# State-space phase: the time steps' two-part weights as one 40-column operand, B by C moved and masked straight from PSUM, one gate product in y's banks

## The reference, cut to what matters

```
proj   = h @ in_proj_w                       # 1024 gate, 1024 ssm, 8 dt, 128 B, 128 C columns
x      = silu(causal_conv4(ssm) + conv_bias) # 8 heads of 128
dt     = softplus(dt_raw + dt_bias);  log_a = -exp(A_log) * dt      # per token and head
L[i,j] = exp(cum[i] - cum[j]) for j <= i, else 0;   CB[i,j] = C[i] . B[j]
y[i]   = sum_j L[i,j] CB[i,j] dt[j] x[j]  +  exp(cum[i]) C[i] @ state
state  = exp(total) state + sum_j exp(total - cum[j]) dt[j] B[j] x[j]
out    = residual + ((y + D x) * silu(gate)) @ out_proj_w
```

## Time and profile before

| | us |
|---|---|
| median of 3 runs | 2466.27 (2464.72 to 2467.67) |
| profiled execution, own time | 2461.78 |
| profiled execution, span from first to last instruction | 2459.9 |
| TensorE busy | 2352.0 (96%) |
| VectorE busy | 1419.1 (58%) |
| ScalarE busy | 957.4 (39%) |
| GpSimd busy | 668.4 (27%) |
| mean granted TensorE clock | 0.985 of full |

### The profile page before, as it was taken

One profiled execution on the slowest core, in us unless ns is written; L12 is line 12 of the kernel. 1 busy time (PEld: TensorE's weight loads), 2 busy tenths in 40 slices (PEclk: granted clock), 3 DMA queues, 4 the chain that ended last, 5 costly groups with the idle time before them and its releaser, 6 DMA issues. The chain is left out here.

```text
span 2459.9 us, 41911 instructions
## 1 busy us (share of the span) xinstructions
PE 2352.0 (96%) x16736; PEld 2074.3 (84%) x16736; DVE 1419.1 (58%) x3237; ACT 957.4 (39%) x1665; POOL 668.4 (27%) x526
## 2 busy tenths in 40 slices
PE   6999999999998999999999999995999999999996
PEld 5999997777787888888888999884999998777775
DVE  5767762222238777777777777765676763222221
ACT  4233332322346444455455555543333231233220
POOL 1244443111121222222222322220144444111121
PEclk9999999999999999999999999997999999999998
DMA  7644225787763111111111111004163413777868
GB/s 250 203 140 155 73 71 174 231 248 235 242 150 104 27 27 27 27 27 26 27 36 35 27 35 27 10 9 158 69 214 105 145 54 104 230 240 230 232 168 171
DMA packets 102754, 292.82 MB, mean 119 GB/s; under 512 B 22498, under 2 KB 22754, under 8 KB 91872
## 3 DMA queue, kind: packets, MB, share of 16 engines
q1 hardware_dynamic: 55216, 198.87, 23.1%
q0 software_dynamic: 47344, 91.27, 16.4%
HBM read 197.28 MB, written 151.80 MB: 142 GB/s over the span
## 5 line engine op out<-in xcount | busy, mean ns | idle before, releaser
L1714 DVE SCALAR_TENSOR_TENSOR m_xt<-m_ssm,m_convw,m_xt 128x256 f32<-128x256 f32 x384 | 219.8, 585 | 57.6 <-ACT m_ssm L1302 48.5
L1425 PE MATMUL m_p_ab<-m_ht_hi,m_wi_b_hi 128*128 128x256 f32 x640 | 183.0, 286 | 3.0 <-ACT m_gate L1274 3.0
L1427 PE MATMUL m_p_ab<-m_ht_hi,m_wi_b_lo 128*128 128x256 f32 x640 | 181.3, 283 | 0.0
L1426 PE MATMUL m_p_ab<-m_ht_lo,m_wi_b_hi 128*128 128x256 f32 x640 | 180.2, 282 | 0.0
L392 POOL DMA_INDIRECT slot_rows<-a_hr,a_slot_now x128 | 130.8, 1022 | 142.3 <-PE p_gate_a L622 85.7
L392 POOL DMA_INDIRECT slot_rows<-b_hr,b_slot_now x128 | 130.5, 1019 | 142.9 <-PE p_gate_b L622 82.8
L620 PE MATMUL p_gate_a<-a_hts_hi,a_w_hi 128*128 128x256 f32 x512 | 148.4, 290 | 7.6 <-DVE a_hts_lo L881 7.4
L620 PE MATMUL p_gate_b<-b_hts_hi,b_w_hi 128*128 128x256 f32 x512 | 148.4, 290 | 7.5 <-DVE b_hts_lo L881 7.4
L620 PE MATMUL p_up_a<-a_hts_hi,a_w_hi 128*128 128x256 f32 x512 | 148.5, 290 | 0.0
L620 PE MATMUL p_up_b<-b_hts_hi,b_w_hi 128*128 128x256 f32 x512 | 148.4, 290 | 0.0
L622 PE MATMUL p_gate_a<-a_hts_hi,a_w_lo 128*128 128x256 f32 x512 | 145.9, 285 | 0.0
(11 more groups left out here) (354 smaller groups left out, 7464.5 us busy)
## 6 DMA issues: line engine op xcount, KB each, us to landing
a_ew<-in_ew SPq DMA_DIRECT2D x32, 1536.0 KB, 7.7
b_ew<-in_ew SPq DMA_DIRECT2D x32, 1536.0 KB, 7.7
after_ffn<-a_zeros POOLq DMA_DIRECT2D x6, 2048.0 KB
out<-b_zeros POOLq DMA_DIRECT2D x6, 2048.0 KB
slot_rows<-a_zeros POOLq DMA_DIRECT2D x1, 8336.0 KB, 40.6
a_rows<-slot_rows SPq DMA_DIRECT2D x32, 260.5 KB, 8.9
b_rows<-slot_rows SPq DMA_DIRECT2D x32, 260.5 KB, 9.0
a_xr<-in_x SPq DMA_DIRECT2D x8, 1024.0 KB, 9.5
```

Source lines behind the costliest of these rows:

```text
L1425: t.matmul(out, l_hi, r_hi_, start=first, stop=False)
L1426: t.matmul(out, l_hi, r_lo_, start=False, stop=False)
L1427: return t.matmul(out, l_lo, r_hi_, start=False, stop=last)
L1714: ins_ = v.scalar_tensor_tensor(xt[:, m, :], ssm[:, m, i:i + BM], convw[:, m, i:i + 1], xt[:, m, :], ALU.mult, ALU.add)
```

## The change

- The weights of dt lie in one operand `w_dt` of 40 columns: high parts in columns 0 to 7, low parts in columns 32 to 39, zeros between (set once by ScalarE in `early`). `project_dt` makes two passes per k-step, with `ht_hi` and with `ht_lo`, 8 matmuls in place of 12. The result has 40 rows, and so has `dtt`.
- `to_tokens` turns dt to tokens by a plain fp32 product with the constant `picks` (40 rows by 8 columns, ones at h and 32 + h), which adds high and low part; the two products stand ahead of the transposes of B and not behind them.
- `b_by_c` stands directly behind `cumulate`, writes into the first bank of `p_y`, and waits for the y of the block before to be read. It is no job any more (21 jobs). VectorE masks it straight from PSUM into `cb`, behind `cum_lo`; ScalarE's copy is gone. `by_cb` and the first `y_product` wait for `cb_ready`.
- Gate 4 goes into the second bank of `p_y`; the other gates alternate in `p_ab` as before. The first `y_product` waits until gate 4 is emptied.
- VectorE's `add_state` of chunk 0 stands ahead of `gated` of chunk 0 and not behind it. For chunk 1 the order stays.

```diff
@@ -1028,10 +1028,13 @@
...
-    JOBS = 6 + 2 * CI
-    J_DT, J_C, J_B, J_TOK, J_CUM, J_CB = 0, 1, 2, 3, 6, 8
-    J_SSM = [4, 5, 7, 9, 10, 11, 12, 13]
-    J_GATE = list(range(14, 22))
+    JOBS = 5 + 2 * CI
+    J_DT, J_C, J_B, J_TOK, J_CUM = 0, 1, 2, 3, 6
+    J_SSM = [4, 5, 7, 8, 9, 10, 11, 12]
+    J_GATE = list(range(13, 21))
+    IN_X, IN_Y = [J_GATE[2], J_GATE[3]], [None, J_GATE[4]]
+    RING = [job for job in range(JOBS) if job not in IN_X + IN_Y]
...
@@ -1043,7 +1046,9 @@
...
-        wi_a = sb("wi_a_hi", [P, KD, SPLIT_COL], F32R), sb("wi_a_lo", [P, KD, SPLIT_COL], F32R)
+        wi_a = sb("wi_a_hi", [P, KD, SPLIT_COL - NH], F32R), sb("wi_a_lo", [P, KD, SPLIT_COL - NH], F32R)
+        w_dt = sb("w_dt", [P, KD, CR], F32R)
...
@@ -1055,7 +1060,7 @@
...
-        dtt = sb("dtt", [NH, BM])
+        dtt = sb("dtt", [CR, BM])
...
@@ -1097,25 +1102,33 @@
...
+            if first == DT0:
+                return w_dt[:, :, 0:NH], w_dt[:, :, LO_AT:CR]
             if first < SPLIT_COL:
-                return [part[:, :, first:first + n] for part in wi_a]
+                return [part[:, :, first - NH:first - NH + n] for part in wi_a]
             i, at = divmod(first - SPLIT_COL, 2 * P)
             return [part[:, i, :, at:at + n] for part in wi_b]
...
-        ab_of = lambda job: p_x[:, job % 2, :] if job in J_GATE[2:4] else p_ab[:, job % 2, :]
+        def ab_of(job):
+            for bank, jobs in ((p_x, IN_X), (p_y, IN_Y)):
+                if job in jobs:
+                    return bank[:, jobs.index(job), :]
+            return p_ab[:, RING.index(job) % 2, :]
...
@@ -1276,7 +1289,7 @@
...
-                copy_job(n, J_DT, dtt[:, :], NH)
+                copy_job(n, J_DT, dtt[:, :], CR)
...
@@ -1320,8 +1333,6 @@
...
                 ssm_job(2)
-                wait(act, decay_ready, n * TM)
-                copy_job(n, J_CB, cb[:, :, :])
...
@@ -1380,6 +1391,8 @@
...
                     act.wait_ge(small_loaded, 96)
                     a.activation(a_neg[:], a_neg[:], ACT.Exp).then_inc(a_exp, 1)
+                    a.activation(w_dt[:, :, NH:LO_AT], c.ones[:, 0:LO_AT - NH].unsqueeze(1).to_broadcast([P, KD, LO_AT - NH]),
+                                 ACT.Copy, scale=0.0).then_inc(gap_set, 1)
...
@@ -1438,19 +1451,34 @@
...
             def ab(n, job):
-                if job in J_GATE[2:4]:
+                if job in IN_X:
                     wait(pe, out_ready, n * TM)
+                elif job in IN_Y:
+                    wait(pe, y_read, n * TM)
                 else:
-                    before = job - 4 if job in J_GATE[4:6] else job - 2
-                    if n * JOBS + before >= 0:
-                        pe.wait_ge(ab_free, n * JOBS + before + 1)
+                    at = RING.index(job)
+                    before = n * JOBS + RING[at - 2] - (JOBS if at < 2 else 0)
+                    if before >= 0:
+                        pe.wait_ge(ab_free, before + 1)
                 return ab_of(job)
-            def project(n, job, col, width=P):
+            def project_dt(n):
                 if is_(n, 0):
-                    pe.wait_ge(w_lo_done, 1 if col == DT0 else (col - NH) // (2 * P) + 2)
-                out = ab(n, job)[0:width, 0:BM]
-                hi, lo = wi(col, width)
+                    pe.wait_ge(w_lo_done, 1)
+                    pe.wait_ge(gap_set, 1)
+                out = ab(n, J_DT)[0:CR, 0:BM]
+                for k in range(KD):
+                    for part in (ht_hi, ht_lo):
+                        mm = t.matmul(out, w_dt[:, k, :], part[:, k, :], start=(k == 0 and part is ht_hi),
+                                      stop=(k == KD - 1 and part is ht_lo))
+                mm.then_inc(ab_full, 1)
+            def project(n, job, col):
+                if is_(n, 0):
+                    pe.wait_ge(w_lo_done, (col - NH) // (2 * P) + 2)
+                out = ab(n, job)[:, 0:BM]
+                hi, lo = wi(col, P)
                 for k in range(KD):
                     mm = three(out, hi[:, k, :], lo[:, k, :],
...
@@ -1460,11 +1488,11 @@
                 pe.wait_ge(ab_free, n * JOBS + J_B + 1)
                 out = ab(n, J_TOK)
                 for j in range(TM):
-                    t.matmul(out[:, j * P:(j + 1) * P], bt[:, j * P:(j + 1) * P], c.ident[:],
-                             is_transpose=True, start=True, stop=True)
+                    at = TM * P + j * NH
+                    t.matmul(out[:, at:at + NH], dtt[:, j * P:(j + 1) * P], c.picks[0:CR, :], start=True, stop=True)
                 for j in range(TM):
-                    at = TM * P + j * NH
-                    mm = t.matmul(out[:, at:at + NH], dtt[:, j * P:(j + 1) * P], c.ident[0:NH, 0:NH],
+                    mm = t.matmul(out[:, j * P:(j + 1) * P], bt[:, j * P:(j + 1) * P], c.ident[:],
                                   is_transpose=True, start=True, stop=True)
                 mm.then_inc(ab_full, 1)
...
@@ -1480,11 +1508,13 @@
...
             def b_by_c(n):
-                out = ab(n, J_CB)
+                if n == 0:
+                    pe.wait_ge(prior.acc_ready, NS * TS)
+                wait(pe, y_read, n * TM)
                 for j in range(TM):
                     tokens = slice(j * P, (j + 1) * P)
-                    mm = t.matmul(out[:, tokens], bt[:, tokens], ct[:, tokens], start=True, stop=True)
-                mm.then_inc(ab_full, 1)
+                    mm = t.matmul(p_y[:, 0, tokens], bt[:, tokens], ct[:, tokens], start=True, stop=True)
+                mm.then_inc(cb_full, 1)
...
@@ -1518,8 +1548,9 @@
                 pe.wait_ge(decay_ready, n * TM + j + 1)
                 pe.wait_ge(cdec_ready, n * TM + j + 1)
                 pe.wait_ge(state_ready, n * TM + j + 1)
-                if n == 0:
-                    pe.wait_ge(prior.acc_ready, NS * TS)
+                if j == 0:
+                    pe.wait_ge(ab_free, n * JOBS + J_GATE[4] + 1)
+                    pe.wait_ge(cb_ready, n + 1)
                 wait(pe, y_read, n * TM + j)
...
@@ -1554,7 +1585,7 @@
             def head(n):
                 pe.wait_ge(ht_ready, n * 2 + 2)
-                project(n, J_DT, DT0, NH)
+                project_dt(n)
                 project(n, J_C, C0)
                 project(n, J_B, B0)
...
@@ -1564,10 +1595,10 @@
                 ssm_part(0)
                 ssm_part(1)
                 cumulate(n)
+                b_by_c(n)
                 if not is_(n, 0):
                     out_product(n - 1, 1)
                 ssm_part(2)
-                b_by_c(n)
                 spread(n, 0)
...
@@ -1692,8 +1723,9 @@
...
             def mask_cb(n):
-                dve.wait_ge(ab_free, n * JOBS + J_CB + 1)
-                link(v.tensor_tensor(cb[:], cb[:], c.upto[:].unsqueeze(1).to_broadcast([P, TM, P]), ALU.mult))
+                dve.wait_ge(cb_full, n + 1)
+                v.tensor_tensor(cb[:], p_y[:, 0, 0:TM * P].rearrange("p (j t) -> p j t", j=TM),
+                                c.upto[:].unsqueeze(1).to_broadcast([P, TM, P]), ALU.mult).then_inc(cb_ready, 1)
...
@@ -1704,6 +1736,7 @@
...
             def by_cb(n, j):
+                dve.wait_ge(cb_ready, n + 1)
                 dve.wait_ge(decay_exp, n * TM + j + 1)
...
@@ -1801,10 +1834,10 @@
...
                     ends(n)
                     cum_lo(n)
+                    mask_cb(n)
                     if n > 0:
                         add_out(n - 1, 1)
                     convolve(n, 2)
-                    mask_cb(n)
                     differences(n, 0)
...
@@ -1828,8 +1861,8 @@
...
                     skip_part(n, 0)
+                    add_state(n, 0)
                     gated(n, 0)
-                    add_state(n, 0)
                     halves(n, 0)
```

More of the change, by code:

```diff
@@ L1112, in mamba @@
         small_loaded, w_hi_done, w_lo_done = sem("small_loaded"), sem("w_hi_done"), sem("w_lo_done")
-        a_exp, set_up = sem("a_exp"), sem("set_up")
+        a_exp, set_up, gap_set = sem("a_exp"), sem("set_up"), sem("gap_set")
         x_loaded, x_stored = [sem(f"x_loaded{u}") for u in range(XM)], [sem(f"x_stored{u}") for u in range(XM)]
@@ L1117, in mamba @@
         t_full, ht_hi_ready, ht_ready = sem("t_full"), sem("ht_hi_ready"), sem("ht_ready")
-        ab_full, ab_free = sem("ab_full"), sem("ab_free")
+        ab_full, ab_free, cb_full, cb_ready = sem("ab_full"), sem("ab_free"), sem("cb_full"), sem("cb_ready")
         nabs_ready, soft_ready, la_ready = sem("nabs_ready"), sem("soft_ready"), sem("la_ready")
```

## The result

The changed kernel takes 2445.97 us (median of 6 runs, 2441.64 to 2449.97), the kernel before 2466.97 in 6 runs beside them. The ratio is 0.9915, with a 95% interval of 0.9897 to 0.9932: faster by 0.85%, 21.0 us, where 15.1 us were forecast. The direction came out as told, and so did most of the mechanisms; the size was missed.

What follows compares the result with a forecast made beforehand. TensorE, busy 56.70 of 57 us, was taken as the bound. Terms -6.9 + 3.8 - 1.3 - 6.2 - 4.0 - 0.5 = -15.1 us gave 2446.7 profiled, 2451.2 us as median forecast, range 2447 to 2455.

Steps and rivals of the forecast that it cites:

- What bounds the kernel: Steady blocks: TensorE busy 56.70 of 57 us; one wait worth naming, chunk 1's y product for the state, 7.5 us.
- Part 1: Dt's product, 12 matmuls to 8: -0.46 us per head, -6.9 us for 15 heads; dearer end -0.13 per head.
- rival B: The 40-column operand of dt's product drains TensorE: +5 us, 2456.2 us; chance 0.15.
- part 4: State ahead of gate: chunk 1's y product no longer waits, -0.41 us per block, -6.2 us; poorer end -0.24.
- Part 2: Dt to tokens, two transposes to two fp32 products ahead of B's transposes: +0.25 us per block, +3.8 us.
- Part 3: B by C moved behind the sums: net -0.08 us per block, -1.3 us; ends -0.2 and +0.1 per block.
- Part 5: Last block: state ahead of gated releases TensorE 2.4 us sooner, clock stays up: -4.0 us, poorer end -2.4.
- Rival C: Y product's stall only changes its owner: 6.5 us less gain, 2457.7 us, with drains 2462.7; chance 0.11.
- Block 0: TensorE's cover is thin; mask and copy lie on the way: -0.5 us, ends -3 and +3.
- Rival D: Gated collides with GpSimd's decayed state, outweighing the gain from 6.5 us; at 7.5 us, 2481 us; chance 0.04.
- Rival E: Drains of Part 2 and Part 3 at cheap ends, or block 0's stall falls: down to 2445; chance 0.05.
- part 6: ScalarE's dropped copy, VectorE's earlier mask, gate 4's bank, two added waits: worth 0 under TensorE's cover; block 0 -0.5 us.

Runs made afterwards that it cites:

- dt alone: Kernel before with only the dt part: 40-column operand, 8 passes, two fp32 products with picks ahead of B's transposes; 2458.24 us, ratio 0.9998.
- the 128-row version: Changed kernel with cum_rows, pick and dtt as 128-row operands, zeros beyond row 40; 2437.1 us, ratio 0.9868 to the kernel before.

## Why the prediction was nearly right and still missed

- **What bounds the kernel**: right. TensorE is full; the one wait that mattered is gone from the steady blocks and no new releaser took its place.
- **Part 1, dt's product**: right, 8 passes at 0.12, nothing for 40 columns; rival B fell. But -0.46 is only collected because part 4 stands with it; alone it went into the stall (dt alone, and the change with gated first). The prediction added the two, and its part 4 had put the 0.46 into the slack (1.8 us), so the sum was right and not by luck; that part 1 alone would be worth nothing it did not say.
- **Part 2, dt to tokens**: right, +0.28 for +0.25. From the output product's second pass back to the last state product pass it is 1.57 us, before 1.29. Of the terms, leaving 40 rows cost 0.18, as estimated 0.20.
- **Part 3, B by C**: 0.00 for -0.08, inside its bounds; -1.3 us that did not come.
- **Part 4, the state first**: right, but priced a little low: -0.41 by the rows, -0.50 in the run that has it alone. 0.07 to 0.08 of the 0.09 between is the y product itself, 3.57 us in place of 3.64, which the sum left out. Rival C fell: nothing else was just behind.
- **Part 5, the last block**: -4.4 for -4.0. The wait is the predicted one; the clock's share is chance, as the same wait in another run shows.
- **Block 0**: missed. From sums to sums the forecast was -0.5 of its own and -0.7 as in every block, together -1.2; measured is -0.9, as much as a steady block won, so nothing is left for a gain of its own.
- **Rival D**: wrong. Gated beside GpSimd's decayed state took 1.47 us, shorter than before, not 6.5. The two do meet, but the decayed state started 0.34 us behind gated, and it is the one that took longer (2.88 us for 1.90), where TensorE doesn't wait for it.
- **Rival E** named 2445, close to what was measured, but by other causes: the cheap ends of parts 2 and 3 and of block 0, none of which came.

The step that failed is part 6, "worth 0" for what the change moves in steady blocks. Its list was of instructions and waits. It left out that two new sizes in SBUF moved the operand that 228 passes a block read, and that is 0.29 us a block by a gap of unused bytes alone, 14 blocks of it 4.1 us. The ledger per block: -0.50 (state first), -0.46 + 0.28 (dt, collected behind it), -0.29 (place), 0 (B by C) = -0.97, measured -0.93; predicted -0.70. Over 14 blocks the miss is 0.23 x 14 = 3.2 us. The place and the y product together went beyond that, and B by C took 0.08 a block back. The other stretches of the profiled executions add 1.4 us of scatter in the unchanged layer, 0.3 in the last block and 0.3 ahead of and behind the blocks, and block 0 takes 0.3 back: 4.9 us in all, -20.0 for -15.1. The range's low end, 2447, had only drains and block 0 behind it. Without the place the median would be near 2450 (an estimate, 2446.0 + 4.1), inside the range; that it fell outside by as little as 1.03 us is also a matter of the scatter.

The Trainium skill, "TensorEngine Tiling (Array Packing)", Key Properties, says that a change of tiling mode drains the engine. If an operand of 40 among 128 is such a change, the runs agree for rows: the 128-row version took away what surrounded the 40-row operands. They show no drain for 40 columns of float32r in part 1, left at 0.12. The prediction took the row there over the page, and this was right.

## What to carry to other kernels

Before pricing a saving on a full engine, look for a wait between it and the end: time saved ahead of a wait comes back as waiting, and the edit that moves the awaited work forward should be priced first, because the others depend on it. An edit that changes a size moves every tensor allocated behind it, and if these are the moving operands of a full TensorE, a gap of 64 to 128 bytes is worth one try on its own, read by the block's period and not by the total. A short operand among full ones can be dearer than a full one with zeros. When TensorE's work shrinks, look at its weight loads and at the spacing of its starts as well: a wait of 0.3 us did not show among TensorE's waits in the waits view.

## What the runs showed of the hardware that I had not expected

- The place in SBUF of a moving float32r operand, and of what is allocated behind it, changes the spacing of its 256-column passes with the same instructions: 119.3 ns at 0, 256 and 512 bytes, 118.0 at 128 and 384, 117.8 at 64, one profile each. Why, and with which other access it meets, is open; with 512 bytes in the changed kernel it was 118.9.
- A run of float32r matmuls with 40 of 128 rows among full ones costs about 0.34 us for in and out together (1.47 against 1.13 us around eight of them); eight float32r matmuls with 40 of 128 columns cost nothing extra (0.12 us from one to the next and to the full one behind).
- The same 1.86 us of idle TensorE was followed by a granted clock of 1.00 in one kernel and, 1.5 us behind it, of 0.50 (1.2 in place of 2.4 GHz) in another, worth 1.6 us.
- VectorE's gated and a GpSimd multiplication over as many elements lengthen one another when they meet, and who pays changes with the order: gated 2.48 us where GpSimd's had started 0.50 us before it, GpSimd's 2.88 in place of 1.90 where gated had started 0.34 us before.
